# A graph kernel's relation edge stage: the chunk's three one-hots as one DVE instruction in place of three on POOL

## The reference

```python
seg = edge_dst * r + edge_type
att = (q[edge_dst] * key_e).sum(-1) * rel_pri[edge_type] / jnp.sqrt(jnp.float32(dk))
amax = jax.ops.segment_max(att, seg, num_segments=S)
ex = jnp.exp(att - amax[seg])
denom = jax.ops.segment_sum(ex, seg, num_segments=S)
hsum = jax.ops.segment_sum(w[:, :, None] * val_e, seg, num_segments=S)   # w = ex / denom[seg]
```

## Time and profile before

| what | us |
|---|---|
| median of 3 runs | 4184.25 (4178.39 to 4203.1) |
| the profiled execution | 4183.35 |
| its span, first to last instruction | 4181.5 |
| `edges_1`: DVE's first `locate` and last `add_acc` start at | 1857.8, 3784.5 |
| busy over the span: PE, DVE | 3689.8, 3607.8 |
| busy over the span: ACT, POOL | 3042.2, 3066.7 |

### The profile page before, as it was taken

One profiled execution on the slowest core, in us unless ns is written; L12 is line 12 of the kernel. 1 busy time (PEld: TensorE's weight loads), 2 busy tenths in 40 slices (PEclk: granted clock), 3 DMA queues, 4 the chain that ended last, 5 costly groups with the idle time before them and its releaser, 6 DMA issues. The chain is left out here.

```text
span 4181.5 us, 116259 instructions
## 1 busy us (share of the span) xinstructions
PE 3689.8 (88%) x23716; PEld 2943.9 (70%) x23717; DVE 3607.8 (86%) x12084; ACT 3042.2 (73%) x9079; POOL 3066.7 (73%) x3573
## 2 busy tenths in 40 slices
PE   4979999999999969979898898998988989886776
PEld 3557777777777758867777677776767777765775
DVE  6878999999999855549999999999999999985887
ACT  3857777777777734439889898888888888883333
POOL 3657777777777634448888888888888888882665
PEclk8989999999999989988888888888888888887999
DMA  3778888888898846657777777777777777784553
GB/s 112 222 231 273 273 277 275 275 276 275 274 275 275 246 151 238 237 201 200 204 206 205 205 204 205 203 206 205 205 206 205 204 205 204 206 187 155 178 174 120
DMA packets 620882, 907.26 MB, mean 217 GB/s; under 512 B 213914, under 2 KB 462794, under 8 KB 620284
## 3 DMA queue, kind: packets, MB, share of 16 engines
q0 software_dynamic: 169984, 585.34, 47.6%
q1 hardware_dynamic: 450812, 321.00, 26.3%
HBM read 734.21 MB, written 175.09 MB: 217 GB/s over the span
## 5 line engine op out<-in xcount | busy, mean ns | idle before, releaser
L901 POOL DMA_INDIRECT kv<-kv_table,rec x864 | 925.6, 1071 | 290.6 <-issue 262.5
L1571 POOL DMA_INDIRECT kv1c<-kv_table,rec x936 | 916.7, 979 | 259.6 <-issue 177.2
L1625 ACT ACTIVATE wv<-kv1c,wv 128x64 f32<-128x64 f32 x3744 | 927.7, 334 | 2.2
L1703 DVE CUSTOM_DVE_ANT_0 masked_scores<-score_p,mask 126x384 f32<-126x384 f32 x1248 | 679.0, 544 | 10.6 <-issue 5.0
L1801 PE MATMUL sum_p<-wv,hot 128*126 128x260 f32 x1872 | 615.9, 476 | 0.9 <-ACT wv L1625 0.9
L1763 PE MATMUL qe_p<-qrel,hotT 126*128 126x256 f32 x1872 | 548.1, 437 | 22.7 <-ACT hotT L1603 16.2
L939 ACT ACTIVATE gates<-gates_p 128x512 f32<-128x512 f32 x864 | 465.6, 591 | 140.8 <-PE gates_p L1071 140.5
L1560 POOL TENSOR_SCALAR hot<-iota,local 128x126 f32<-128x126 f32 x936 | 549.2, 600 | 0.2
L1763 PEld LDWEIGHTS qe_p<-qrel,hotT 126*128 126x128 f32 x1872 | 428.4, 229 | 109.7 <-ACT hotT L1603 16.4
L1801 PEld LDWEIGHTS sum_p<-wv,hot 128*126 128x126 f32 x1872 | 391.0, 223 | 85.8 <-ACT wv L1625 1.7
L1090 PE MATMUL sum_p<-msg,hot_weighted 128*126 128x256 f32 x1728 | 433.7, 394 | 5.1 <-ACT hot_weighted L947 5.1
(11 more groups left out here) (277 smaller groups left out, 8291.4 us busy)
## 6 DMA issues: line engine op xcount, KB each, us to landing
key<-segment_keys SPq DMA_DIRECT2D x312, 189.0 KB
q_blk<-q_table SPq DMA_DIRECT2D x216, 192.5 KB
acc_table<-acc SPq DMA_DIRECT2D x312, 128.0 KB
qrel<-q_by_relation SPq DMA_DIRECT2D x312, 126.0 KB
feat<-in_edge_feat_t SPq DMA_DIRECT2D x216, 128.0 KB
agg_and_x_plus_h<-total SPq DMA_DIRECT2D x216, 126.0 KB
kv1c<-kv_table,rec POOLq DMA_INDIRECT x936
kv<-kv_table,rec POOLq DMA_INDIRECT x864
```

Source lines behind the costliest of these rows:

```text
L901: pool.indirect_dma_start(kv[it.slot(AHEAD)][:, t, :], None, c["kv0_d"], bass.IndirectOffsetOnAxis(ap=rec[k][:, t, 0:1].bitcast(I32), axis ...
L1571: pool.indirect_dma_start(kv[k][:, t, :], None, c["kv1_d"], bass.IndirectOffsetOnAxis(ap=rec[k][:, t, 0:1].bitcast(I32), axis=0)).then_inc ...
L1625: ins = act.activation(wv[k][:, t, h, 0:DK], kv[s][:, t, D + h * DK:D + (h + 1) * DK], ACT.Copy, scale=wv[k][:, t, h, DK:DK + 1])
L1703: dve.tensor_tensor_reduce(junk[k][:, h, :], score_p[:, h, :], mask[it.slot(4)][:], 1.0, -BIG, ALU.add, ALU.max, top[s][:, h:h + 1]).then_ ...
```

## The change

`locate` and its tile `local` go. `one_hot` leaves POOL and becomes one `scalar_tensor_tensor` on DVE, (iota + par) == key over 128 x 3 x 126 with iota and key broadcast, in f32, at lag 0. It stands between `new_peak` and `peak_drop`.

```diff
-        local = [sb(f"local1{k}", [P, T1]) for k in range(2)]
...
-                def one_hot(it):
-                    hold(pool, held, local_ready, it.count())
-                    wait(pool, summed, it, U)
-                    pool.sem_inc(held, 1)
-                    for t in range(T1):
-                        ins = pool.tensor_scalar(hot[it.slot(U)][:, t, :], c["iota"][:],
-                                                 local[it.slot(2)][:, t:t + 1], None, ALU.is_equal)
-                    ins.then_inc(hot_ready, 1)
...
-                run_chunks(pool, steps, ((5, fade_acc), (1, one_hot), (0, gather)))
+                run_chunks(pool, steps, ((5, fade_acc), (0, gather)))
...
-                def locate(it):
+                def one_hot(it):
                     s = it.slot(U)
                     wait_slot(dve, loaded, it, LOADS)
-                    wait(dve, hot_ready, it, 2)
-                    dve.tensor_scalar(local[it.slot(2)][:], rec[s][:, :, 2], par[s][:, 1:2], None,
-                                      ALU.subtract).then_inc(local_ready, 1)
+                    wait(dve, summed, it, U)
+                    dve.scalar_tensor_tensor(hot[s][:],
+                                             c["iota"][:].rearrange("p (o n) -> p o n", o=1).to_broadcast([P, T1, SEG]),
+                                             par[s][:, 1:2], rec[s][:, :, 2:3].to_broadcast([P, T1, SEG]),
+                                             ALU.add, ALU.is_equal).then_inc(hot_ready, 1)
...
-                run_chunks(dve, steps, ((2, q_times_k), (4, below_peak), (2, scores), (4, cap), (0, locate),
+                run_chunks(dve, steps, ((2, q_times_k), (4, below_peak), (2, scores), (4, cap),
...
-                                        (3, old_peak), (5, add_acc), (3, new_peak), (3, peak_drop)))
+                                        (3, old_peak), (5, add_acc), (3, new_peak), (0, one_hot), (3, peak_drop)))
```

More of the change, by code:

```diff
@@ L1483, in edges_1 @@
         loaded, gathered = sems("edge1_loaded", U), sems("kv1_gathered", U)
-        dist_ready, mask_ready, local_ready, hot_ready, hotT_ready = sem("dist1"), sem("mask1"), sem("local1"), sem("hot1"), sem("hotT1")
+        dist_ready, mask_ready, hot_ready, hotT_ready = sem("dist1"), sem("mask1"), sem("hot1"), sem("hotT1")
         qe_ready, qk_ready, score_ready = sem("qe1"), sem("qk1"), sem("score1")
```

## The result

The changed kernel takes 4167.41 us (median of 20 runs, 4158.91 to 4212.2) where the kernel before, run beside it, takes 4186.89 (20 runs, 4178.39 to 4233.42). The ratio is 0.995, 95% interval 0.9926 to 0.9973: about 20 us less, within the 1% that was called no change. The forecast was 4158. The profiled execution took 4167.31 us, its span 4165.5.

A forecast was written before the change was run, and what follows sets the result against it. The prediction took POOL, full at 6.09 us a step, as the bound. DVE's terms gave 5.96 us, with 0.05 us of PE waits 6.01; 0.08 x 312 = 25 us less made 4158 us, range 4040 to 4235.

The forecast's parts named there:

- the hold: In `edges_1`, DVE's compare and POOL's multiply exclude each other, making `peak_drop` late by 0.37 us a step; chance 0.66.
- the sum: DVE's terms for one `edges_1` step: 5.96 us, with waits for PE 6.01 us against 6.09 before.
- POOL was the bound, and stops being it: In `edges_1`, POOL is full at 6.09 us a step; without its three compares, 1.76 us, it needs 4.33.
- The compare: On DVE between `new_peak` and `peak_drop`: 0.53 us slot, 0.61 us duration, 0.43 us added to the step.
- The half rate rule: Rival: DVE's compare runs at half throughput, 0.40 us more, step 6.41 us, 4283 us; chance 0.04.
- The other signs that it named: `fade_acc` about 1.1 us or late, waiting for `add_acc` in most steps; `cap` under 0.3 us; DVE idle under 0.1 us.
- `cap` held: On DVE, POOL's gathers can hold `cap` between 0 and 0.42 us; 0.10 us a step was taken.
- the waits for PE: I keep 0.05 us: DVE's `qk` comes 0.43 + 0.37 us later behind PE's turn, so most waits go and 0.05 us stays.
- The rival without a hold, 4049 us: The hold hardly comes: DVE needs 5.49 us, with 0.17 us of waits 5.66 us a step, 134 us less; chance 0.16.
- the lower end of the range: For the launch time, 4040 us, set so that the case of no hold lies inside.
- POOL's readiness: Loads land 7.8 us behind `add_acc`; POOL is ready for the next `fade_acc` after 5.4 us and waits 0.6 us.

The follow-up runs named there:

- four runs that turn it off at `peak_drop`: Changed kernel with compare ahead of `old_peak` (1.0088), behind `cap` at lag 0 (1.003) or lag 1 (0.9915), or with POOL's multiply moved to DVE (1.0326).
- one that moves it to the compare: Changed kernel with the compare behind `peak_drop` instead of before it: 4180.11 us, ratio 0.9969 to the kernel before.
- the version behind `q_times_k`: Changed kernel with the compare directly behind `qk`, for the chunk of lag 1: 4153.52 us, ratio 0.9906 to the kernel before.
- Three kernels with `peak_drop` free: Changed kernel with the lag 1 compare behind `cap` (4155.02 us) or `q_times_k` (4153.52); kernel before with two POOL compares removed, zeros written by POOL (4169.93).
- the best two versions: Changed kernel with the compare at lag 1, behind `q_times_k` (4153.52 us, ratio 0.9906) or behind `cap` (4155.02 us, 0.9915).

## Why the prediction came true, point by point

The change of 20 us against 25 forecast has the right sign and nearly the right size, and the hold was foreseen. That the sum came out is in part luck all the same: it adds the hold's 0.37 us to the length of the step, and where the hold was taken away DVE's work fell by 0.27 us a step and the step by only 0.05 to 0.08. No version came under 5.95 us a step, with a hold or without, and the sum met that limit from another side.

**POOL was the bound, and stops being it.** Right: the earlier trace rows against 3.65 us a step, and its distances from `fade_acc` to `fade_acc` have a standard deviation of 0.90 us where it was 0.03. The kernel with one compare on POOL shows the same, and that the bound stood only 0.05 us above the next.

**The compare.** Right: 0.61 us, computed from the earlier trace rows; from `new_peak` to `peak_drop` it is now 0.59 us, computed 0.61. The half rate rule of the Trainium skill, page Vector Engine (DVE) Microarchitecture Reference, section Points that are easy to get wrong, doesn't hold for this instruction: the trace doesn't agree, at 0.60 to 0.61 us for 378 f32 columns with two SBUF sources.

**The hold.** Right in mechanism and order, in four runs that turn it off at `peak_drop` (0.177, 0.172, 0.176 and 0.155 us) and one that moves it to the compare; and in size for the step that was computed. Computed: the multiply comes 0.19 us behind `add_acc`, measured 0.18; it takes 0.27 us more, measured 0.26; `peak_drop` late by 0.37, with a duration of 0.58 and `qk` 0.51 behind it where 0.57 was computed. The 0.57 is 0.20 unheld and 0.37 of hold; by the 54 free steps without a wait it is 0.07 unheld, so the hold costs DVE 0.43 and two errors cancel. What the prediction did not have is the second form, in which POOL is still in its last gather: 68 steps, with the longer hold. The other signs that it named came out in part: `cap` and the compare as said; waits of `fade_acc` for `add_acc` in 102 of 298 steps and not in most, with a multiply of 0.758 us in the mean and not 1.1; DVE idle for 0.24 us and not under 0.1.

**The sum, and where it was wrong.** 6.01 us was computed and 6.03 measured, but two errors of about 0.26 us met. From the undisturbed step above, in us:

| term | computed | measured |
|---|---|---|
| `qk` to `cap` | 1.86 | 1.85 |
| `cap` to first `maxima`, with `cap` held | 0.13 + 0.10 | 0.07 |
| `maxima` to `add_acc`, to `new_peak` | 2.35 + 0.34 | 2.35 + 0.34 |
| `new_peak` to `peak_drop` | 0.18 + 0.43 | 0.59 |
| `peak_drop` to `qk` | 0.20 + 0.37 | 0.51 |
| sum without waits | 5.96 | 5.71 |
| waits and disturbed steps | 0.05 | 0.32 |

`cap` is hardly held: over 0.3 us in 6 of 100 steps. Its phase to the gathers lay as computed, and I still put 0.10 on it. The step that failed is "the waits for PE: I keep 0.05 us". I argued that `qk` comes later behind PE's turn, which is true: its waits fell from 56.5 to 26.9 us. But DVE waits for PE at the `maxima` and `diff` too, and a long step is a loss for good now. Before, POOL's beat of 6.09 us left DVE 0.43 us of slack a step with which it caught up behind each long step (7.05, 5.51, 5.86, 5.97 us is such a run). After, DVE has none. DVE's idle time by the profile is 0.24 us a step, of which 26.9 + 13.8 + 3.8 = 44.5 us in all, or 0.15 a step, stand against PE by name. The rest lies in held instructions (`peak_drop` up to 1.08 us), less what the steps without a hold save, and in gaps that I did not follow. The failure is one of principle as well as of size: the hold and the waits for PE were added as if each came on top of the other, but without the hold the waits grow by nearly what it cost.

**The rival without a hold, 4049 us.** Its DVE part, 5.49 us, was too long: the undisturbed 5.71 less 0.43 is 5.28, and the shortest of the free steps take 5.27. (The 5.47 of the version behind `q_times_k` is another place of the compare, where nothing hides behind it.) Its waits, 0.17 us, should have been 0.45 and more. Three kernels with `peak_drop` free and 5.2 to 5.5 us of DVE work come out at 5.95 to 6.04 us a step, and none has a median below 4153 us, so nothing here came near this rival's time, and the lower end of the range was set too low. That PE's lower clock and the loads are the cause in common fits the waits and the clock ahead of the long steps, but no run took either away cleanly; it is not shown.

**POOL's readiness.** I had the gather start as the last load lands. When POOL has been idle it starts 0.87 us behind it, and where a gather waited for loads (209 times) they had landed 8.26 us behind `add_acc` in the median, not 7.8. So POOL is often not ready for the meeting 5.4 us after the last. With a little lateness it meets `peak_drop` all the same, in the second form above; with more it doesn't, and in 23 of 100 steps `peak_drop` isn't held. The times of the multiply part the two kinds without an exception: up to 0.46 us behind the start of `peak_drop` in the held steps, 0.91 and more in the free ones.

## What to carry to other kernels

When an engine with a fixed beat sets the pace, measure how far below it the next limit lies, with all its waits and not by its busy time, before paying anything to relieve it: here POOL lost 1.76 us a step and the step got 0.06 of it. A hold read off one engine's timeline is that engine's cost and not the launch's: here it was 0.43 us a meeting, and taking it away took 0.05 to 0.08 us off the step. Where a DVE instruction with two SBUF inputs can meet a POOL one that the same event releases, as the compare met the multiply here, the order decides which instruction pays. Put it where it delays neither its follower nor an engine that waits, and give it a lag at which its loads have landed; here that gave the best two versions, 12 to 14 us under the kernel after, with intervals that overlap.

## What the runs showed of the hardware that I had not expected

- Eight more DVE instructions, executed once ahead of the loop, took the instruction queue from 59 packets to 239 and made DVE stand for 5.4 us in each pass, the launch 3.6% longer. With the same eight on POOL the queue stayed at 59 and no stall came.
- PE with less to do is granted less: 0.62 to 0.65 against 0.85 with all its matmuls in the same set of runs, and its busy time a step went up from 5.72 to between 5.89 and 6.06 us with four matmuls fewer.
- The hold reaches ahead of the record of POOL's multiply, up to half a us into the gather before it (143 of 143 cases in two kernels, 22 of 34 in a third), and `peak_drop` in the kernel after then takes 0.84 us in the mean instead of 0.58.
- An indirect DMA on POOL starts 0.87 us behind the landing it waited for when POOL is idle (median of 209).
- The instruction held at the port gets going before the record of the other one ends, 0.13 to 0.2 us, if its unheld duration is counted back from its end. The Trainium skill, page SBUF — State Buffer, section SBUF: two separate sides, has the loser fully blocked for the whole instruction; by the records it is a little less.
